# Attention probabilities: scaled in place by VectorE and GpSimd and then transposed, instead of multiplied by a diagonal matrix

## The reference, cut to what matters

```python
q = rmsnorm((hidden_states @ Wq).reshape(B, Sq, H, D), gq)
k = rmsnorm((encoder_hidden_states @ Wk).reshape(B, Skv, H, D), gk)
scores = jnp.einsum('bqhd,bkhd->bhqk', q, k) * scale
attn = jax.nn.softmax(scores, axis=-1)
out = jnp.einsum('bhqk,bkhd->bqhd', attn, v)
return out.reshape(B, Sq, H * D) @ Wo
...
energy = jnp.einsum('bnd,bmd->bnm', query, key)
attention = jax.nn.softmax(energy, axis=-1)
x_m = jnp.einsum('bln,bmn->blm', teacher_logits, attention)
```

## Time and profile before

| | before |
|---|---|
| time, median of 3 runs | 1267.17 us (1266.77 to 1268.74) |
| the profiled execution's span | 1266.5 us |
| mean granted TensorE clock | 0.81 |
| TensorE busy | 866.9 us (68%) |
| VectorE busy | 813.6 us (64%) |
| ScalarE busy | 498.3 us (39%) |
| GpSimd busy | 330.0 us (26%) |
| row maxima L1697 | 68, mean 0.689 us, 29.4 us idle before them |

### The profile page before, as it was taken

How to read it: one execution, slowest core, us unless ns; L and a number is a source line. 1 busy time by engine, 2 the same in 40 slices (tenths; PEclk the granted TensorE clock), 3 DMA queues, 4 the chain that set the end, 5 groups by cost and what they waited for, 6 DMA issues and landing times.

```text
span 1266.5 us, 16161 instructions
## 1 busy us (share of the span) xinstructions
PE 866.9 (68%) x4324; PEld 657.8 (52%) x4324; DVE 813.6 (64%) x2012; ACT 498.3 (39%) x1242; POOL 330.0 (26%) x344
## 2 busy tenths in 40 slices
PE   2114863587348842884588997969789797879756
PEld 1003631565136621762375785749667595658635
DVE  4896789569875888468430776348653676438653
ACT  3331422233122421252147445545365453555332
POOL 4744462326221643122020002120023001130023
PEclk9555975799558955896689997989899897989857
DMA  3150000010001000112300000010000100000000
GB/s 128 66 230 13 0 1 1 1 46 0 0 0 46 0 0 0 67 67 104 121 30 12 2 5 1 1 35 1 5 0 0 35 1 5 0 21 1 1 1 9
DMA packets 12190, 33.48 MB, mean 26 GB/s; under 512 B 2121, under 2 KB 5585, under 8 KB 10321
## 3 DMA queue, kind: packets, MB, share of 16 engines
q1 hardware_dynamic: 12112, 32.70, 7.3%
HBM read 30.59 MB, written 2.10 MB: 26 GB/s over the span
## 4 chain that ended last, share of the span: by engine, by line
issue 51%; DVE 18%; PE 14%; POOL 11%; ACT 3%; DMA 1%; DVEq 1%; POOLq 1%; SPq 0%; ACTq 0%
PE bk L944 13%; DVE pool L1497 2%; POOL acl L591 2%; POOL pool L559 2%; DVE pool L1503 2%; POOL ac L597 2%; DVE t L1523 1%; DVE pool L1489 1%; DMA pool<-in_wo 1%; POOL lnr L531 1%; POOL fside L619 1%; POOL q7bd L619 1%; DVE v L1636 1%; POOL ac L572 1%; POOL v L581 1%
## 5 line engine op out<-in xcount | busy, mean ns | idle before, releaser
L559 POOL TENSOR_TENSOR pool<-pool 128x512 f32<-128x512 f32 x64 | 94.1, 1470 | 124.4 <-DVE pool L1503 124.0
L531 POOL TENSOR_TENSOR lnr<-lnv,mhalf 128x2 f32<-128x2 f32 x20 | 16.9, 845 | 419.0 <-DVE lnv L1402 418.7
L1523 DVE SCALAR_TENSOR_TENSOR t<-th,bk 128x256 f32<-128x256 f32 (+1 forms) x120 | 50.1, 417 | 107.6 <-ACT th L760 106.5
L944 PE MATMUL bk<-hT,first 128*128 128x256 f32 (+1 forms) x448 | 113.2, 400 | 0.0
L751 ACT ACTIVATE ssm_da<-m,nega 128x255 f32<-128x255 f32 x128 | 57.7, 499 | 118.5 <-DVE pool L1497 104.9
L944 PE MATMUL bk<-early,first 128*128 128x256 f32 x384 | 96.5, 389 | 0.0
L944 PEld LDWEIGHTS bk<-hT,first 128*128 128x128 f32 (+1 forms) x448 | 87.9, 200 | 15.7 <-issue 1.0
L944 PE MATMUL bk<-bc,sel 96*128 96x512 bf16 (+1 forms) x128 | 52.8, 419 | 58.6 <-DVE pool L1503 45.6
L1497 DVE TENSOR_TENSOR_SCAN pool<-ssm_da,pool 128x512 f32<-128x512 f32 x64 | 90.2, 1409 | 0.4
L944 PE MATMUL bk<-first,ac 128*128 128x256 f32 (+1 forms) x224 | 65.2, 416 | 28.9 <-POOL ac L572 28.9
L760 ACT ACTIVATE th<-bk 128x256 f32<-128x256 f32 x88 | 33.9, 385 | 127.1 <-PE bk L944 126.8
(11 more groups left out here) (353 smaller groups left out, 2381.7 us busy)
## 6 DMA issues: line engine op xcount, KB each, us to landing
out<-xo SPq DMA_DIRECT2D x8, 256.0 KB, 2.6
pool<-in_wo SPq DMA_DIRECT2D x4, 512.0 KB, 4.6
first<-in_wq SPq DMA_DIRECT2D x1, 2048.0 KB, 9.0
first<-in_wd SPq DMA_DIRECT2D x1, 1792.0 KB, 16.6
first<-in_wg SPq DMA_DIRECT2D x1, 1760.0 KB, 8.6
first<-in_wu SPq DMA_DIRECT2D x1, 1760.0 KB, 12.3
xin<-in_x SPq DMA_DIRECT2D x4, 256.0 KB, 3.0
pool<-in_q3u SPq DMA_DIRECT2D x1, 1024.0 KB, 5.1
```

The lines of the kernel that those rows point to most:

```text
L531: g.tensor_tensor(lnr, lnv, mhalf[:, 0:2], ALU.pow).then_inc(*sig(f"{k}.pool", "lnr"))
L559: g.tensor_tensor(sy, sy, ssm_u[:, n % 3, :].rearrange("p (e t) -> p e t", e=2), ALU.add).then_inc(*sig("s0.pool", "y", n))
L944: return t_.matmul(dst, lhsT, rhs, start=start, stop=stop)
L1523: v.scalar_tensor_tensor(out=quarter(t1, c)[0:m, :], in0=quarter(th, c)[0:m, :], scalar=1.0, in1=bank[0:m, 0:S], op0=ALU.add, op1=ALU.mult ...
```

## The change

The diagonals go. After the reciprocal, VectorE scales block t = 0 of the exponentials in place (one 128x256 multiplication by a column of `rd`), and GpSimd scales block t = 1 in place (one 128x256 product with the column broadcast). TensorE's `probsT` then does four true transposes with `ident`: two after VectorE's block, two after GpSimd's. VectorE's wait for `probsT` of head j - 3 goes, since the diagonal buffer is gone. GpSimd gets an attention loop of 16 such instructions per batch, and one more in `s6`.

```diff
@@ GpSimd
+            def normalise(b, k, j):
+                pool.wait_ge(*at(b, f"{k}.dve", "rd", j))
+                pm = pm4[j % 3][:, 1, :]
+                g.tensor_tensor(pm, pm, rd4[:, j, 1:2].broadcast_to([P, S]), ALU.mult).then_inc(*sig(f"{k}.pool", "pn", j))
+
+            def attention(b):
+                for j in range(NH):
+                    normalise(b, "sa", j)
...
             def s6(b):
                 yield AT6["ln"]
                 ln(b, "s6")
+                yield AT6["exp"]
+                normalise(b, "s6", 0)
...
             def phase_b(b, ahead):
+                attention(b)
@@ TensorE
             def probsT(b, k, j):
-                pe.wait_ge(*at(b, f"{k}.dve", "dg", j, 1))
                 if j >= 2:
                     pe.wait_ge(*at(b, "sa.dve", "pl", j - 2, 1))
-                bank, slot = (PTB[j % 2], j % 3) if k == "sa" else (MB, 2)
-                for kc in range(2):
-                    for t in range(2):
-                        i = mm(bank[:, kc * S + t * P:kc * S + t * P + P], pm4[j % 3][:, t, kc * P:kc * P + P], dg4[slot][:, t, :])
+                bank = PTB[j % 2] if k == "sa" else MB
+                for t, half in enumerate(("dve", "pool")):
+                    pe.wait_ge(*at(b, f"{k}.{half}", "pn", j))
+                    for kc in range(2):
+                        i = t_.transpose(bank[:, kc * S + t * P:kc * S + t * P + P], pm4[j % 3][:, t, kc * P:kc * P + P], ident[:, :])
                 i.then_inc(*sig(f"{k}.pe", "pt", j))
@@ VectorE, rden
                 v.reciprocal(rd4[:, j, :], den4[:, n, :]).then_inc(*sig(f"{k}.dve", "rd", j))
                 dve.wait_ge(*at(b, f"{k}.dve", "rd", j))
-                if j >= 3:
-                    dve.wait_ge(*at(b, f"{k}.pe", "pt", j - 3))
-                for t in range(2):
-                    v.tensor_scalar(dg4[j % 3 if k == "sa" else 2][:, t, :], ident[:, :], rd4[:, j, t:t + 1], None, ALU.mult).then_inc(*sig(f"{k}.dve", "dg", j, t))
+                pm = pm4[j % 3]
+                v.tensor_scalar(pm[:, 0, :], pm[:, 0, :], rd4[:, j, 0:1], None, ALU.mult).then_inc(*sig(f"{k}.dve", "pn", j))
```

More of the change, by code:

```diff
@@ L170, in build @@
         pm_extra, e0 = cut(first, e0, 2, S)
-        dg_extra, e0 = cut(first, e0, 2, P)
         q37 = [sb(f"q37{n}", [P, W2], F32R) for n in "ugd"]
@@ L282, in build @@
         pm4 = [two(t) for t in th] + [pm_extra]
-        dg4 = [cut(da_flat, S * i, 2, P)[0] for i in range(2)] + [dg_extra]
         pT4 = [two(t) for t in t1]
```

## The result

| | before | after |
|---|---|---|
| time, median | 1266.97 us (1266.61 to 1268.74) | 1251.53 us (1249.66 to 1252.29) |
| ratio | | 0.9872, 95% interval 0.9860 to 0.9884 |
| span of the profiled execution | 1266.5 us | 1249.6 us |
| mean granted TensorE clock | 0.81 | 0.81 |

A forecast was written before the change was run, and what follows sets the result against it. TensorE was taken to bound the steady heads. Span 1266.5 less 24.5 for four attentions and 1.4 for s6 gave 1240.6, plus 0.7 made 1241 us; range 1231 to 1258, 8 in 10.

The forecast's parts named there:

- the forecast: Whole kernel: 1241 us, own range 1235 to 1247, chance 0.69.
- the clock: Rival: TensorE's clock falls, one head in each attention at 1.2 GHz costing 3.0 us more; 1253 us, chance 0.06.
- the cheaper transposes: Rival: fp32 transposes at the price of bf16 ones, 0.056 us apart; 1231 us, chance 0.05.
- VectorE held by GpSimd: Rival: in the scaling GpSimd is first and holds VectorE until it ends; circle 3.20, 1263 us, chance 0.10.
- TensorE: 64 attention heads: probsT from 0.89 to 0.46 us, 0.43 saved, a steady head 3.01 us.
- VectorE's circle, 2.62: Loop from maximum through VectorE and ScalarE to next maximum: 2.75 less 0.13 is 2.62 us, below TensorE's 3.01.
- Who gets the way into SBUF: Scaling halves after the reciprocal: VectorE starts first by 0.04 us and is not held; GpSimd waits a little.
- only move forward: DMA, phase A and the stages other than attention and s6: nothing is changed in them, so no saving.
- s6: One-head stage, four times: 0.35 us saved each, bounds −0.5 and +0.4; four give 1.4 us.
- nor did they cost as much as the products: Rival: transposes cost as much as products, only early heads and s6 gain; 1262 us, chance 0.04.
- GpSimd never made a steady head's transposes wait: Steady heads: TensorE's new wait for GpSimd's half costs nothing, slack 1.2 us; transposes waiting there would show it wrong.
- `nb` stayed at 0.16: Sign against the forecast: VectorE's negated maximum over 0.2 us, held by GpSimd; it was expected just behind GpSimd's end.

The follow-up runs named there:

- e2: Changed kernel, but GpSimd's half waits for VectorE's half instead of for the reciprocal; 1239.69 us, ratio 0.9776.
- e4: Changed kernel with the scaling by the reciprocals left out on both engines, so probabilities are not normalised; 1229.48 us.
- e8: Changed kernel, but ScalarE scales the second half instead of GpSimd, and VectorE keeps its own; 1236.53 us, ratio 0.9750.
- e10: Changed kernel, but ScalarE scales the second half in the 16-head attention, VectorE both halves in s6, GpSimd none; 1235.83 us, ratio 0.9746.
- e1: Changed kernel, but VectorE scales both halves, one 128x256 instruction each, and GpSimd none; 1236.01 us, ratio 0.9746.
- e3: Changed kernel with the scaling kept, but fp32 products with ident in place of the transposes; 1270.41 us.
- e6: Changed kernel with GpSimd's instruction twice as wide, into its own buffer, waiting from head 2 on for probsT of head j - 2; 1249.04 us.
- e9: Changed kernel with one more GpSimd wait, from head 2 on for probsT of head j - 2, its instruction unchanged; 1245.71 us.

## Why the prediction came out as it did

The time lies in the stated range, but by luck: that range took in the forecast, the clock and the cheaper transposes, while the case that came, VectorE held by GpSimd, had been priced at 1263 us, outside it. It fell inside because GpSimd's instruction was shorter than assumed (0.61 us for 0.73) and two other stages shrank.

**TensorE.** Right. 0.44 us for the transposes for 0.89 (predicted 0.46), a TensorE head of 2.98 to 2.99 (predicted 3.01), seen in e2, e4, e8, e10, in TensorE's own spacing in e1 and in e3's 3.44 without the transposes.

**VectorE's circle, 2.62.** Right for the kernel without the hold: e2 and e8 have it to the hundredth. Wrong for the changed kernel, where it is 3.07.

**Who gets the way into SBUF.** This is the step that failed. Its first half was right: VectorE's record does start first, by 0.043 us (predicted 0.04), in all 68 scalings. The second half, "I take it that it is not held", is what the runs overturned. The earlier trace rows could not carry it: there VectorE came second, or was well ahead (the pair's first instruction starts at 182.97, GpSimd's at 183.21, 0.24 later), so they showed that the later one waits, never that a lead of 0.04 us protects the earlier one. The changed kernel shows that it doesn't; e6 and e9 show that 0.11 does.

The trace of before has closer pairs, which the prediction did not look at. In phase A a bf16 copy of VectorE starts 0.053 to 0.059 us ahead of GpSimd in three of the four batches:

```profile
280.93 0.28 DVE L1461 COPY bc<-bcmid 32x512 bf16<-32x512 bf16 x1
280.98 1.59 POOL L545 TENSOR_SCALAR m<-m 128x512 f32<-128x512 f32 x1 [0.27 <-DVE bc L1460]
```

There VectorE takes 0.28 (0.45 in the remaining batch, where GpSimd is 0.18 ahead), and GpSimd's record grows to 1.58 or 1.59 from the 1.49 that it has without the copy. In these three places of all twelve traces the copy leads by 0.049 to 0.063 and is never held. So a lead of 0.049 was enough for this copy and one of 0.045 was not for the scaling. These rows would have spoken for the forecast; but the scaling's lead is smaller than the copy's, and the instruction is another one. A margin of 0.04 us should have had more than the 0.10 that I gave the rival.

**The price.** The rival for this case said circle 3.20 and 1263 us (with the 0.7 that the forecast adds at its end, its sum is nearer 1264). Its mechanism was right in all but who starts first. Its size was off by one term: GpSimd's product with a broadcast column takes 0.61 us, not the 0.73 of L591. With 0.61 the hold is 0.45 and the circle 2.62 + 0.45 = 3.07, as measured; fifteen heads are then 46.1, not 48.0. That is 1.9 us in each of four batches, 7.6 of the 11.5 us between 1263 and the time; the rest is mostly the next point.

**Other stages "only move forward".** Not quite: `s5` lost 2.0 us and the turn to the next attention 2.0. The `s5` stretch depends on how long TensorE's clock stays at its lower level behind the attention's residual: from 759.8 to 773.4 us before, from 760.2 to 770.4 after. In the first three batches of all kernels the level rises again 13.1 to 16.3 us after that residual, and the stage takes 35.3 to 36.9 us with it: 13.2 and 35.33 in the second batch of after, 15.9 and 36.67 in the first of before. Which batch gets which is in no fixed order, so I read it as alignment and not as an effect. The turn is steadier: 9.40 and 9.64 before, 8.39 to 8.67 in after, e1, e2 and e9. Near its end VectorE waits for nothing that the profile shows, for 3.45 us before and 2.56 after:

```profile
843.52 0.42 DVE L1749 TENSOR_TENSOR acl<-cx,ach 128x256 fp32r<-128x256 f32 x1 [3.45 <-issue]
```

```profile
839.79 0.43 DVE L1758 TENSOR_TENSOR acl<-cx,ach 128x256 fp32r<-128x256 f32 x1 [2.56 <-issue]
```

(Both are VectorE's timeline at the first turn, of the kernel before and of after.) e3 turns in 8.42 with products instead of transposes and e1 in 8.49 without GpSimd, so it goes with what all of them lack, VectorE's diagonals and their wait. It is not the number of VectorE's instructions: e1 has as many as before, 2012. Why, no run told; it stays open.

**`s6`.** 1.1 us for 1.4: the first three save 0.18 each, not 0.35. The later half ends 1.01 after the start of `rd` (798.36), close to the 1.1 I had for GpSimd, but then 0.75 us pass until ScalarE's copy, not 0.5: VectorE's held half ends last, and all four transposes come behind it. The last batch saves 0.56.

**The other rivals.** The clock did not fall in the loop: it is 1.00 from 702.2 us to behind the residual in the first batch, and likewise in the others once it has risen. But it rose later in the second batch, 6.2 us after maximum 0 where before it was 2.1; there the early heads had room for it, and their periods are 3.07 as everywhere. (The Trainium skill, TensorE: Matmul & The Clock Gate, Part 4, says that transposes don't engage the full clock as products do. Four among 19 records of a head did nothing to it here.) The transposes did not get cheaper than 0.11 apart, nor did they cost as much as the products. GpSimd never made a steady head's transposes wait. `nb` stayed at 0.16, since GpSimd has ended by then.

**Signs.** Of the signs named, the first batch's VectorE half at 0.80 us decided at once against "not held"; it was the sign the prediction gave for "GpSimd first" (0.9), with the period 3.07 for its 3.2.

## What to carry to other kernels

Don't split a scaling like this one between VectorE and GpSimd on SBUF operands at the same release: here the halves ran one after the other, and the faster engine paid for the slower one's whole instruction (0.81 us for 0.35). Give both halves to VectorE, one to ScalarE, or let GpSimd wait for VectorE's end. True transposes in place of fp32 products with a diagonal halved TensorE's time for them (0.44 us for 0.89), which paid even though the scaling had to be done separately. And a lead of a few hundredths of a us in the records says nothing of the order in which two engines get in, unless the same pair of instructions has been seen at that lead: price the case in which it fails as likely.

## What the runs showed of the hardware that I had not expected

- **A start 0.04 us ahead doesn't win.** This VectorE fp32 scaling, SBUF to SBUF, when its record starts 0.042 to 0.045 us before that of GpSimd's instruction, is held until 0.15 after that one's end (0.81 us with GpSimd at 0.61, 1.23 with 1.04). From 0.11 us ahead it takes its own 0.35, and GpSimd's record grows instead, 0.61 to 0.72. The bf16 copy L1461 has its way from 0.049 ahead. (By the rule of the Trainium skill, SBUF — State Buffer, section SBUF: two separate sides, whichever starts first has the way in and the other fully blocks. The blocking agrees; "first" isn't the order of the records' starts here. Whether VectorE asks for its way in only some hundredths after its record begins, no run tells.)
- **GpSimd's 128x256 product with a broadcast column is cheaper than with two full inputs,** 0.612 us against 0.732 for L591 and 0.722 at the least for L572, and the 128x512 form takes 1.04.
- **With VectorE's hold gone and GpSimd later, TensorE's low clock shows.** In e2 the second period of batches 1 and 2 is 3.27 us, with `mx` idle 0.57 for TensorE, where batches 0 and 3 have 2.62. Busy time by stretch of e2, head 1 to head 2 in batch 0 and in batch 1 (columns as above):

```profile
703.09:705.71 2.62, 1.86 (x9) 1.16 (x9) 1.64 (x7) 1.71 (x6) 0.61 (x1) 1.00 0.00 0
...
842.10:845.37 3.27, 3.12 (x10) 2.18 (x11) 1.73 (x6) 1.75 (x6) 1.10 (x2) 0.50 0.00 0
```

The clock is at its lower level for one head longer in batch 1. TensorE's transposes of head 0 wait there for GpSimd's late half, the scores of head 2 come behind them at the lower level, and the maximum waits for those (timeline of e2, a weight load and the maximum):

```profile
842.93 0.29 PEld L1177 LDWEIGHTS bk<-ident,th 128*128 128x128 f32 x2 [0.40 <-POOL th L632]
...
845.37 0.69 DVE L1708 TENSOR_REDUCE mx<-bk 128x2 f32<-128x512 f32 x1 [0.57 <-PE bk L955]
```

Both causes have a part: at the same low clock in the same place e8, whose second half is ready sooner, has a period of 3.00, and e1 has its usual 2.88. In the changed kernel the clock is low there too, and the 3.07 of the hold hides it.
